# Layer-1 attention: projections over four PSUM banks, spreading products and their copies in the MLP

## The chip, the cores and the metric

The kernel runs on one core of a Trainium2 chip. The metric is the device time of one execution, in microseconds (us). The engines are PE (TensorE), ACT (ScalarE), DVE (VectorE), POOL (GpSimd) and SP (which issues DMAs).

## The reference

Two transformer layers on x of 16 sequences x 512 tokens x 256 features, each stage added to x: linear attention with a memory, a routed MLP, the stage of this document, and a top-1 routed MLP. The stage of this document, for each sequence (`LN` is a layer norm):

```
h  = LN(LN(x)) * ln1_g + ln1_b
q, k, v = heads(h @ WQ + bQ), heads(h @ WK + bK), heads(h @ WV + bV)   # 16 heads of 16
attn = softmax(q k^T / 4, causal, window of 128 keys)
u = h @ Bw;  s_t = A * s_(t-1) + u_t;  ssm = s @ Cw                    # 64 states
g = sigmoid(h @ Wg + bg)
x1 = LN(x) + g * ((attn v) @ WO + bO) + (1 - g) * ssm
out = x + x1 + gelu(LN(x1) @ W1 + b1) @ W2 + b2                        # 1024 hidden
```

## The kernel before, in words

The stage is attn1_phase. Each engine has its own program, written out by hand; the order within an engine is the order of the code, and engines wait for each other by semaphores (`pe.wait_ge(q4_ready, ...)`; `after` is the same, left out where its value isn't positive). A loop `body(it)` runs over 16 sequences. Products in float32 are made of three products of halves, a hi and a lo part each (the helper `three`, lines 72 to 74): wherever PE's result is used as an operand again, ACT copies the hi part out of PSUM and DVE makes the lo part by a subtraction. In what follows that pair is called a split.

PE's body for one sequence has these parts:
- Score steps n = 0 to 31, two heads by 128 queries each. scores(n) writes a mask and q k^T into one of the two banks of s_ps; DVE takes the maximum (maxima), ACT the exponential (exp, two heads, each with a sum), POOL normalises (normalise), PE transposes three steps later (transposes), ACT copies (pT_copy), and PE multiplies by v two steps after that (values). scores(n) waits for exp(n - 2). Steps 0 to 7 have 128 keys, the others 256. After n = 17, 25, 33 and at the end stands a mix: output projection and state product of 128 tokens, 14 products, which ACT copies and POOL gates into x1.
- Spreading. scores needs q and k of a head alone in its rows: spread_qk(j), j = 0 to 7, multiplies q and k by 0/1 matrices, two products for each (hi and lo), into two banks of ab_ps; ACT copies q (q4_copy), DVE copies k (k4_copy). spread_qk 0 and 1 stand ahead of step 0, the others in steps 0 to 5, each ahead of its scores. One bank for each of q and k: spread_qk(j) waits for the copies of j - 1.
- After the scores, for the next sequence: h_transposes, four queries_keys (q and k by halves of 128 features), four values_gates (by 128 tokens, v and gate in one product), and state_input, followed by DVE's scan over the tokens. They use ab_ps[0] and ab_ps[1] in turn, so each waits for the split or eviction of the one before the last.
- h2_transposes after the second layer norm: DVE statistics (stats2_of, norm2), POOL the deviation (inverse_deviation2), DVE normalises (h2n_of).
- The MLP: eight chunks of 128 hidden features. mlp1(m) writes ab_ps[m % 2], ACT applies gelu and copies hi, DVE makes lo, mlp2(m) adds into y_ps, which is the same memory as s_ps. mlp1 runs two chunks ahead. Then DVE adds y to the residual (result_of, four parts).

ACT evaluates the gate's tanh (gates) at the start of a sequence's body, then loads the table for the exponential.

Of the kernel before, what the change touches and what calls it, by code (L numbers as in the profile page):

```python
# [1305 lines left out]
def attn1_phase(nc, x, out, wqk_d, wvg_d, bw_d, cw_d, wo_d, w1_d, w2_d, spread_d, cols_d, rows_d, b1_d, a_d, window_d, half_d, ident_d):  # L1306
# [7 lines left out]
    with ExitStack() as ctx:  # L1314
# [110 lines left out]
        y_ps = s_ps[:].rearrange("p s h k -> p (s h) k")  # L1425

# [187 lines left out]
        def _(act):  # L1614
# [9 lines left out]
            def qk_hi(it, a, m):  # L1624

                act.wait_ge(q_in_psum, (it * 2 + a) * DC + 2 - m)

                after(act, k4_in_psum, it * PAIRS1)
                nc.scalar.activation(qk_hl[a][0][:, m], ab_ps[:, m], ACT.Identity, bias=(bq, bk)[a][:, m:m + 1]).then_inc(qhi_ready, 1)

            def q4_copy(it, j):
                act.wait_ge(q4_in_psum, it * PAIRS1 + j + 1)
                after(act, s_ready, it * NS)
                nc.scalar.copy(q4[:, j], ab_ps[:, 0]).then_inc(q4_ready, 1)
# [69 lines left out]
            projections(0)  # L1704

            def body(it):
                gates(it)

                nc.scalar.activation(table[:], b1[:, 0:1], ACT.Exp)
                q4_copy(it, 0)  # L1710
                q4_copy(it, 1)
                for n in range(NS + LAG_T):
                    if n + 2 < PAIRS1:
                        q4_copy(it, n + 2)
# [20 lines left out]
                for c in range(DC):  # L1735
                    h2_hi(it, c)
                for m in range(MF):
                    gelu(it, m)
                    ff_hi(it, m)

# [3 lines left out]
        def _(dve):  # L1744
# [37 lines left out]
            def qk_lo(it, a, m):  # L1782

                dve.wait_ge(qhi_ready, (it * 2 + a) * DC + 2 - m)
                nc.vector.scalar_tensor_tensor(qk_hl[a][1][:, m], ab_ps[:, m], (bq, bk)[a][:, m:m + 1], qk_hl[a][0][:, m].bitcast(F32), ALU.add, ALU.subtract).then_inc(qlo_ready, 1)

            def values_gates(it, t):
# [5 lines left out]
                nc.vector.tensor_tensor(v[:, t, :, 0:DH1], heads(ab_ps[:, t % 2, 0:D]), heads(rows[:, 0]), ALU.add)  # L1793
                nc.vector.tensor_tensor(gate[:, t], ab_ps[:, t % 2, D:2 * D], rows[:, 1], ALU.add).then_inc(vg_ready, 1)

            def k4_copy(it, j):
                dve.wait_ge(k4_in_psum, it * PAIRS1 + j + 1)
                after(dve, s_ready, it * NS)
                nc.vector.tensor_copy(k4[:, j], ab_ps[:, 1]).then_inc(k4_ready, 1)
# [70 lines left out]
            def projections(it, part):  # L1870
                if part == 0:
                    for a, m in ((0, 0), (1, 1), (1, 0)):
                        qk_lo(it, a, m)
                    values_gates(it, 0)
                    values_gates(it, 1)
                else:
                    values_gates(it, 2)
                    values_gates(it, 3)
                    scan(it)

# [6 lines left out]
            qk_lo(0, 0, 1)  # L1887
            projections(0, 0)
            projections(0, 1)
# [867 lines left out]
```

## Time and profile before

| | us |
|---|---|
| median of 3 runs | 5219.56 (5172.9 to 5221.64) |
| the profiled execution | 5248.13 |
| its span | 5246.3 |
| mean granted TensorE clock | 0.928 |
| PE busy | 4322.6 (82%) |
| DVE, ACT, POOL busy | 2994.6, 2465.0, 2300.0 |

The stage of this change runs from about 2655 to 4880 us of the span. Busy time of different engines overlaps; idle time counts only where it is on the way to the end. A clock of 1.00 is 2.4 GHz, 0.50 is 1.2 GHz.

### The profile page before, as it was taken

What the parts mean: (1) busy time and instruction counts of PE and PEld (TensorE: products, weight loads), DVE (VectorE), ACT (ScalarE), POOL (GpSimd) and SP (SyncE); (2) the same over time, 40 slices, a digit from 0 to 9 for tenths busy, and PEclk for the clock granted to TensorE, in tenths of its full rate; (3) what the DMA queues carried; (4) which work ended last, traced back from release to release, by engine and by line L of the source; (5) the groups of instructions that cost most, each with busy time, mean ns of one, the idle gap of its engine ahead of it and who ended that gap; (6) DMA issues with size and microseconds to landing.
All of it is one profiled execution on the core that took longest, in us unless ns stands there. A gap on an engine that the chain in (4) does not pass through costs nothing. (4 is left out here: it accounts for less than half of the span.)

```text
span 5246.3 us, 152203 instructions
## 1 busy us (share of the span) xinstructions
PE 4322.6 (82%) x61044; PEld 3367.0 (64%) x61140; DVE 2994.6 (57%) x7226; ACT 2465.0 (47%) x5553; POOL 2300.0 (44%) x2391
## 2 busy tenths in 40 slices
PE   3888898888888868888858988888888888888556
PEld 3776776676677757777746666566666656666555
DVE  3777777777767657777654344444444444443444
ACT  3554545554544423323325455555555555555334
POOL 4666666666656400000004444444444444443443
PEclk8999999999999989999979799899999989999579
DMA  2212212222221110000010000000000000000332
GB/s 82 52 44 62 64 47 56 65 49 53 63 56 44 42 51 17 24 24 16 24 60 9 1 8 8 8 8 8 8 8 8 8 8 8 8 8 5 120 96 91
DMA packets 151975, 186.91 MB, mean 36 GB/s; under 512 B 28254, under 2 KB 112353, under 8 KB 149985
## 3 DMA queue, kind: packets, MB, share of 16 engines
q1 hardware_dynamic: 144528, 160.98, 11.4%
q0 software_dynamic: 6864, 17.99, 0.9%
q8 instruction: 388, 6.36, 0.5%
q14 instruction: 195, 1.59, 0.1%
HBM read 68.48 MB, written 44.19 MB: 21 GB/s over the span
## 5 line engine op out<-in xcount | busy, mean ns | idle before, releaser
L1571 POOL TENSOR_TENSOR c_prob<-c_prob,c_inv 128x512 f32<-128x512 f32 (+1 forms) x512 | 484.1, 952 | 825.8 <-DVE c_inv L1824 807.5
L1654 ACT ACTIVATE c_prob<-c_s_ps,c_nmax 128x256 f32<-128x256 f32 (+1 forms) x1024 | 454.2, 453 | 312.0 <-DVE c_nmax L1819 304.9
L1819 DVE TENSOR_REDUCE c_nmax<-c_s_ps 128x2 f32<-128x512 f32 (+1 forms) x512 | 317.4, 620 | 404.8 <-PE c_s_ps L2021 401.6
L848 POOL TENSOR_TENSOR a_swap<-a_swap,a_sin 128x512 f32<-128x512 f32 x128 | 203.0, 1586 | 563.0 <-DMA a_swap<-a_raw 563.0
L2033 PE MATMUL c_t_ps<-c_ident,c_prob 128*128 128x128 f32 x1792 | 321.6, 298 | 14.3 <-POOL c_prob L1571 12.7
L889 ACT COPY a_raw<-a_w_ps 128x512 f32<-128x512 f32 x256 | 150.3, 587 | 350.4 <-PE a_w_ps L74 350.0
L212 POOL TENSOR_TENSOR b_var<-b_mv,b_eps 128x4 f32<-128x4 f32 x16 | 8.5, 533 | 695.4 <-DVE b_mv L304 695.3
L1665 ACT COPY c_pT<-c_t_ps 128x512 f32<-128x512 f32 (+1 forms) x512 | 276.7, 540 | 56.9 <-PE c_ab_ps L2051 55.0
L1170 PE MATMUL a_w_ps<-a_mem,a_sT 64*32 64x65 f32 x14848 | 216.2, 226 | 100.3 <-issue 96.8
L2021 PE MATMUL c_s_ps<-c_k,c_q 64*128 64x256 f32 (+1 forms) x1024 | 257.8, 333 | 22.8 <-issue 20.1
L1170 PEld LDWEIGHTS a_w_ps<-a_mem,a_sT 64*32 64x32 f32 x14848 | 170.2, 106 | 152.1 <-issue 131.1
L1860 DVE TENSOR_TENSOR c_ff_lo<-c_ff,c_ff_hi 128x512 fp32r<-128x512 f32 x128 | 88.6, 692 | 299.9 <-ACT c_ff_hi L1695 299.9
L252 ACT ACTIVATE b_s_sb<-b_gu_ps 128x512 f32<-128x512 f32 x144 | 86.1, 598 | 368.2 <-PE b_gu_ps L74 368.2
L72 PE MATMUL a_w_ps<-a_xT_hi,a_wqk_hi 128*128 128x512 f32 x512 | 237.2, 463 | 20.9 <-DVE a_x_ln L968 12.9
L72 PE MATMUL b_y_ps<-b_wd_hi,b_h_hi 128*128 128x256 f32 x576 | 176.7, 307 | 93.9 <-DVE b_acc L406 47.2
L2033 PEld LDWEIGHTS c_t_ps<-c_ident,c_prob 128*128 128x128 f32 x1792 | 196.9, 146 | 83.1 <-POOL c_prob L1571 16.6
L72 PE MATMUL b_gu_ps<-b_xT_hi,b_wgu_hi 128*128 128x512 f32 x576 | 234.2, 407 | 10.7 <-DVE b_xT_lo L373 10.7
L73 PE MATMUL b_gu_ps<-b_xT_hi,b_wgu_lo 128*128 128x512 f32 x576 | 232.1, 403 | 0.0
L2021 PEld LDWEIGHTS c_s_ps<-c_k,c_q 64*128 64x128 f32 x1024 | 157.9, 193 | 112.4 <-issue 97.1
L74 PE MATMUL b_gu_ps<-b_xT_lo,b_wgu_hi 128*128 128x512 f32 x576 | 229.8, 399 | 0.0
L73 PE MATMUL a_w_ps<-a_xT_hi,a_wqk_lo 128*128 128x512 f32 x512 | 220.0, 430 | 2.8 <-issue 2.8
L74 PE MATMUL a_w_ps<-a_xT_lo,a_wqk_hi 128*128 128x512 f32 x512 | 219.4, 429 | 3.4 <-issue 3.2
(377 smaller groups left out, 13836.9 us busy)
## 6 DMA issues: line engine op xcount, KB each, us to landing
a_swap<-a_raw SPq DMA_DIRECT2D x1024, 64.0 KB, 2.1
d_xb<-sorted_rows SPq DMA_DIRECT2D x71, 130.0 KB
a_x_ln<-x SPq DMA_DIRECT2D x128, 64.0 KB, 2.1
a_acc<-x SPq DMA_DIRECT2D x64, 128.0 KB, 2.8
after_attn<-a_acc SPq DMA_DIRECT2D x64, 128.0 KB, 2.4
b_x_in<-after_attn SPq DMA_DIRECT2D x16, 512.0 KB, 4.4
after_ffn<-b_acc SPq DMA_DIRECT2D x16, 512.0 KB, 3.2
c_x_in<-after_ffn SPq DMA_DIRECT2D x16, 512.0 KB, 4.2
```

What stands on the lines that cost most here:

```text
L72: nc.tensor.matmul(out, w[0], x[0], start=start, stop=False, **options)
L73: nc.tensor.matmul(out, w[1], x[0], start=False, stop=False, **options)
L74: return nc.tensor.matmul(out, w[0], x[1], start=False, stop=stop, **options)
L848: nc.gpsimd.tensor_tensor(q_sw, q_sw, table(sin), ALU.mult)
L889: (rawq_ready, rawk_ready)[a].by(nc.scalar.copy(raw[:, m % 3, a], bank))
L1170: ins = nc.tensor.matmul(into[s * SEG:(s + 1) * SEG, r, j], sT[d, (n // T * T + j) % (2 * PU), a, tok], mem[d, s, j], start=True, stop=True)
L1571: nc.gpsimd.tensor_tensor(p, p, inv[:, n % 4].unsqueeze(2).to_broadcast([P, 2, KB])[:, :, keys_of(i)], ALU.mult).then_inc(norm_ready, 1)
L1654: last = nc.scalar.activation(prob[:, n % 4, h, keys_of(i)], s_ps[:, n % 2, h, keys_of(i)], ACT.Exp, bias=nmax[:, n % 4, h:h + 1], accum_o ...
L1665: nc.scalar.copy(pT[:, n % 2, :, b[0]:2], t_ps[:, n % 2, :, b[0]:2]).then_inc(pT_ready, 1)
L1819: nc.vector.tensor_reduce(nmax[:, n % 4], s_ps[:, n % 2, :, keys_of(i)], AX.X, ALU.max, negate=True).then_inc(max_ready, 1)
L2021: last = nc.tensor.matmul(s_ps[:, n % 2, h, keys_of(i)], q4[r4, slot, i * P:(i + 1) * P], k4[r4, slot, keys_], start=False, stop=(h == 1), ...
L2033: last = nc.tensor.transpose(t_ps[:, n % 2, h, b], prob[:, n % 4, h, b * P:(b + 1) * P], ident[:])
```

## The change

- in_ps: the four query/key products and the four values_gates products use four banks in turn, ab_ps[1], ab_ps[0] and the two banks of s_ps, which the scores have left by then.
- The spreading products use two other banks, o_ps for q and c_ps for k. Those of the next sequence are issued in the MLP: j = 0 ahead of mlp1(0), 1 to 5 after the chunks m = 0 to 4, 6 and 7 after m = 6 and 7. Their copies stand at the same places on ACT and DVE. For the first sequence all eight stand ahead of the loop.
- gates (tanh) of the next sequence stands after chunk 6 of the MLP, the table load for the exponential before the last q4_copy.
- On DVE, splits and evictions of the next sequence are spread between the steps of the second layer norm; on PE, state_input now stands ahead of h2_transposes, and values_gates 2 and 3 behind them.
- scores 0 waits for two of the four results of the sequence before, scores 1 for all.

The diff, with context and the loss of one helper (DVE's projections) left out; "more" is "not last_step(it)":

```diff
@@ -1423,6 +1423,11 @@
 y_ps = s_ps[:].rearrange("p s h k -> p (s h) k")
+s_bank = [s_ps[:, k].rearrange("p h k -> p (h k)") for k in range(2)]
+in_ps = [ab_ps[:, 1], ab_ps[:, 0], s_bank[0], s_bank[1]]
+in_order = ((0, 1), (0, 0), (1, 1), (1, 0))
+q4_ps = o_ps[:]
+k4_ps = c_ps[:].rearrange("p a d -> p (a d)")
...
@@ -1626,12 +1631,12 @@
         after(act, k4_in_psum, it * PAIRS1)
-        nc.scalar.activation(qk_hl[a][0][:, m], ab_ps[:, m], ACT.Identity, bias=(bq, bk)[a][:, m:m + 1]).then_inc(qhi_ready, 1)
+        nc.scalar.activation(qk_hl[a][0][:, m], in_ps[in_order.index((a, m))], ACT.Identity, bias=(bq, bk)[a][:, m:m + 1]).then_inc(qhi_ready, 1)
...
         after(act, s_ready, it * NS)
-        nc.scalar.copy(q4[:, j], ab_ps[:, 0]).then_inc(q4_ready, 1)
+        nc.scalar.copy(q4[:, j], q4_ps).then_inc(q4_ready, 1)
...
@@ -1702,16 +1707,13 @@
     projections(0)
+    for j in range(PAIRS1):
+        q4_copy(0, j)
+    gates(0)
+    nc.scalar.activation(table[:], b1[:, 0:1], ACT.Exp)
     def body(it):
-        gates(it)
-        nc.scalar.activation(table[:], b1[:, 0:1], ACT.Exp)
-        q4_copy(it, 0)
-        q4_copy(it, 1)
         for n in range(NS + LAG_T):
-            if n + 2 < PAIRS1:
-                q4_copy(it, n + 2)
...
@@ -1734,9 +1736,20 @@
             h2_hi(it, c)
+        if not last_step(it):
+            q4_copy(it + 1, 0)
...
             ff_hi(it, m)
+            if not last_step(it):
+                if 1 <= m < MF - 2:
+                    q4_copy(it + 1, m)
+                if m == MF - 2:
+                    gates(it + 1)
+        if not last_step(it):
+            q4_copy(it + 1, PAIRS1 - 2)
+            nc.scalar.activation(table[:], b1[:, 0:1], ACT.Exp)
+            q4_copy(it + 1, PAIRS1 - 1)
...
@@ -1782,7 +1795,7 @@
         dve.wait_ge(qhi_ready, (it * 2 + a) * DC + 2 - m)
-        nc.vector.scalar_tensor_tensor(qk_hl[a][1][:, m], ab_ps[:, m], (bq, bk)[a][:, m:m + 1], qk_hl[a][0][:, m].bitcast(F32), ALU.add, ALU.subtract).then_inc(qlo_ready, 1)
+        nc.vector.scalar_tensor_tensor(qk_hl[a][1][:, m], in_ps[in_order.index((a, m))], (bq, bk)[a][:, m:m + 1], qk_hl[a][0][:, m].bitcast(F32), ALU.add, ALU.subtract).then_inc(qlo_ready, 1)
...
@@ -1790,13 +1803,13 @@
         heads = lambda ap: ap.rearrange("p (h e) -> p h e", e=DH1)
-        nc.vector.tensor_tensor(v[:, t, :, 0:DH1], heads(ab_ps[:, t % 2, 0:D]), heads(rows[:, 0]), ALU.add)
-        nc.vector.tensor_tensor(gate[:, t], ab_ps[:, t % 2, D:2 * D], rows[:, 1], ALU.add).then_inc(vg_ready, 1)
+        nc.vector.tensor_tensor(v[:, t, :, 0:DH1], heads(in_ps[t][:, 0:D]), heads(rows[:, 0]), ALU.add)
+        nc.vector.tensor_tensor(gate[:, t], in_ps[t][:, D:2 * D], rows[:, 1], ALU.add).then_inc(vg_ready, 1)
...
         after(dve, s_ready, it * NS)
-        nc.vector.tensor_copy(k4[:, j], ab_ps[:, 1]).then_inc(k4_ready, 1)
+        nc.vector.tensor_copy(k4[:, j], k4_ps).then_inc(k4_ready, 1)
...
@@ -1884,17 +1886,18 @@
         h_lo(0, c)
-    qk_lo(0, 0, 1)
-    projections(0, 0)
-    projections(0, 1)
+    for part in in_order:
+        qk_lo(0, *part)
+    for t in range(T):
+        values_gates(0, t)
+    scan(0)
+    for j in range(PAIRS1):
+        k4_copy(0, j)
...
         order.step(it)
-        k4_copy(it, 0)
-        k4_copy(it, 1)
+        more = not last_step(it)
         for n in range(NS + 1):
-            if n + 2 < PAIRS1:
-                k4_copy(it, n + 2)
...
@@ -1917,24 +1920,40 @@
         ao_lo(it, T - 1)
-        if not last_step(it):
+        if more:
...
         stats2_of(it, T - 2)
-        if not last_step(it):
-            projections(it + 1, 0)
+        if more:
+            qk_lo(it + 1, 0, 0)
+            qk_lo(it + 1, 1, 1)
...
         norm2(it)
+        if more:
+            qk_lo(it + 1, 1, 0)
+            values_gates(it + 1, 0)
         h2n_of(it)
-        if not last_step(it):
-            projections(it + 1, 1)
+        if more:
+            values_gates(it + 1, 1)
+            scan(it + 1)
...
             affine(it, c, tab[c], h2T, ln2_g, ln2_b, h2T_in_psum, h2T_ready)
+        if more:
+            values_gates(it + 1, 2)
...
             h2_lo(it, c)
+        if more:
+            values_gates(it + 1, 3)
+            k4_copy(it + 1, 0)
...
             ff_lo(it, m)
+            if more and 1 <= m < MF - 2:
+                k4_copy(it + 1, m)
+        if more:
+            k4_copy(it + 1, PAIRS1 - 2)
...
             result_of(it, t)
+        if more:
+            k4_copy(it + 1, PAIRS1 - 1)
...
@@ -1955,7 +1974,7 @@
             pe.wait_ge(hn_ready, it + 1)
-            after(pe, k4_ready, it * PAIRS1)
+            after(pe, ff_ready, (it - 1) * MF)
...
@@ -1965,15 +1984,16 @@
-    def queries_keys(it, a, m):
-        if a:
-            pe.wait_ge(qlo_ready, it * 2 * DC + (2 - m))
-        elif m:
+    def queries_keys(it, n):
+        a, m = in_order[n]
+        if n == 0:
             pe.wait_ge(hlo_ready, (it + 1) * DC)
-        else:
+        elif n == 1:
             after(pe, aolo_ready, it * T)
-        feature_major(wqk, slice(a * D + m * P, a * D + (m + 1) * P), hT_hl, ab_ps[:, m]).then_inc(q_in_psum, 1)
+        elif n == 2:
+            after(pe, exp_ready, it * NS)
+        feature_major(wqk, slice(a * D + m * P, a * D + (m + 1) * P), hT_hl, in_ps[n]).then_inc(q_in_psum, 1)
...
@@ -1981,23 +2001,21 @@
-            pe.wait_ge(vg_ready, (it + 1) * T)
-            after(pe, ff_ready, it * MF)
-        for a, (full, free) in enumerate(((q4_in_psum, q4_ready), (k4_in_psum, k4_ready))):
+            pe.wait_ge(qlo_ready, (it + 1) * 2 * DC)
+        for a, (bank, full, free) in enumerate(((q4_ps, q4_in_psum, q4_ready), (k4_ps, k4_in_psum, k4_ready))):
...
                 pe.wait_ge(free, it * PAIRS1 + j)
+            elif a:
+                pe.wait_ge(state_ready, it + 1)
             for half_ in range(2):
-                last = nc.tensor.matmul(ab_ps[:, a], spread[:, jj, 2 * a + half_], qk_hl[a][half_][:, c], start=(half_ == 0), stop=(half_ == 1))
+                last = nc.tensor.matmul(bank, spread[:, jj, 2 * a + half_], qk_hl[a][half_][:, c], start=(half_ == 0), stop=(half_ == 1))
...
     def values_gates(it, t):
-        if t < 2:
-            pe.wait_ge(qlo_ready, (it * 2 + 1) * DC + 2 - t)
-        else:
-            pe.wait_ge(vg_ready, it * T + t - 1)
+        pe.wait_ge(qlo_ready, it * 2 * DC + t + 1)
...
         for c in range(DC):
-            last = three(nc, ab_ps[:, t % 2], [h[:, c, tok] for h in hT_hl], [w[:, c] for w in wvg], c == 0, c == DC - 1)
+            last = three(nc, in_ps[t], [h[:, c, tok] for h in hT_hl], [w[:, c] for w in wvg], c == 0, c == DC - 1)
...
@@ -2010,7 +2028,9 @@
             pe.wait_ge(k4_ready, it * PAIRS1 + 2 * (n // 2) + 2)
-        if n == 0:
+        if n == 0 and not first_step(it):
+            pe.wait_ge(result_ready, it * T - T // 2)
+        elif n == 1:
...
@@ -2041,10 +2061,12 @@
-            if i == 1:
+            if i == 0:
                 pe.wait_ge(q4_ready, (it + 1) * PAIRS1)
+            elif i == 1:
+                after(pe, ff_ready, it * MF)
             else:
-                after(pe, aolo_ready, it * T + i - 1)
+                pe.wait_ge(aolo_ready, it * T + i - 1)
...
@@ -2058,6 +2080,7 @@
             pe.wait_ge(statelo_ready, it + 1)
+            pe.wait_ge(k4_ready, (it + 1) * PAIRS1)
...
@@ -2077,7 +2100,8 @@
         if m < 2:
-            pe.wait_ge(vg_ready, (it + 2) * T if not last_step(it) else NSEQ * T)
+            if not last_step(it):
+                pe.wait_ge(vg_ready, (it + 1) * T + 2)
...
@@ -2086,8 +2110,10 @@
-            pe.wait_ge(exp_ready, (it + 1) * NS)
+            if last_step(it):
+                pe.wait_ge(exp_ready, NSEQ * NS)
+            else:
+                pe.wait_ge(vg_ready, (it + 2) * T)
...
@@ -2096,18 +2122,17 @@
         h_transposes(0, c)
-    for a, m in ((0, 1), (0, 0), (1, 1), (1, 0)):
-        queries_keys(0, a, m)
+    for n in range(2 * DC):
+        queries_keys(0, n)
...
     state_input(0)
+    for j in range(PAIRS1):
+        spread_qk(0, j)
     def body(it):
-        spread_qk(it, 0)
-        spread_qk(it, 1)
+        more = not last_step(it)
         for n in range(NS + LAG_P):
-            if n + 2 < PAIRS1:
-                spread_qk(it, n + 2)
...
@@ -2118,26 +2143,28 @@
                 h_transposes(it + 1, (n - 27) // 3)
-        if not last_step(it):
-            queries_keys(it + 1, 0, 1)
+        if more:
+            queries_keys(it + 1, 0)
         mix(it, T - 1)
-        if not last_step(it):
-            queries_keys(it + 1, 0, 0)
-            queries_keys(it + 1, 1, 1)
-            queries_keys(it + 1, 1, 0)
+        if more:
+            for n in range(1, 2 * DC):
+                queries_keys(it + 1, n)
...
             values_gates(it + 1, 1)
+            state_input(it + 1)
+        h2_transposes(it)
+        if more:
             values_gates(it + 1, 2)
-        h2_transposes(it)
-        if not last_step(it):
             values_gates(it + 1, 3)
-            state_input(it + 1)
+            spread_qk(it + 1, 0)
...
                 mlp1(it, m + 2)
+            if more and m != MF - 3:
+                spread_qk(it + 1, m + 1 if m < MF - 3 else m)
```

## Rows read from the trace of the kernel before

**Rows 1.** Busy time by window, three stretches of one sequence; columns in its first line.

```profile
core 0: us, PE busy (x) PEld busy (x) DVE busy (x) ACT busy (x) POOL busy (x), PEclk, DMA share, GB/s
...
3637.30:3669.70 32.40, 23.41 (x91) 17.35 (x89) 13.76 (x30) 7.95 (x12) 16.19 (x20) 0.84 0.00 0
3669.70:3690.40 20.70, 19.94 (x132) 18.10 (x133) 4.84 (x7) 9.47 (x15) 0.00 (x0) 1.00 0.00 1
3690.40:3695.80 5.40, 3.51 (x15) 1.91 (x13) 2.71 (x6) 3.72 (x6) 0.00 (x0) 1.00 0.48 138
```

**Rows 2.** Timeline, ACT: start us, length us, operation; the tanh of six of 16 sequences.

```profile
2746.92 1.06 ACT L1639 ACTIVATE c_gate<-c_gate 128x1024 f32<-128x1024 f32 x1 [7.53 <-DVE c_gate L1794]
...
3028.44 1.06 ACT L1639 ACTIVATE c_gate<-c_gate 128x1024 f32<-128x1024 f32 x1 [2.27 <-issue]
...
3288.35 1.06 ACT L1639 ACTIVATE c_gate<-c_gate 128x1024 f32<-128x1024 f32 x1 [2.21 <-issue]
...
3430.83 1.06 ACT L1639 ACTIVATE c_gate<-c_gate 128x1024 f32<-128x1024 f32 x1 [1.95 <-issue]
...
3690.09 1.06 ACT L1639 ACTIVATE c_gate<-c_gate 128x1024 f32<-128x1024 f32 x1 [1.95 <-issue]
...
4740.31 1.05 ACT L1639 ACTIVATE c_gate<-c_gate 128x1024 f32<-128x1024 f32 x1
```

**Rows 3.** Busy time by window, the three long stretches at the low clock.

```profile
2897.00:2950.00 53.00, 51.68 (x228) 30.59 (x229) 17.48 (x47) 26.50 (x84) 26.22 (x32) 0.50 0.00 1
3312.00:3342.00 30.00, 29.15 (x130) 17.78 (x132) 9.91 (x29) 14.12 (x46) 15.47 (x21) 0.51 0.00 0
4234.00:4262.00 28.00, 27.18 (x118) 16.29 (x118) 9.15 (x27) 13.53 (x43) 14.98 (x20) 0.50 0.00 0
```

**Rows 4.** Timeline, PE, from projections to MLP; idle time before and releaser in brackets.

```profile
3637.31 0.50 PE L72 MATMUL c_ab_ps<-c_hT_hi,c_wqk_hi 128*128 128x512 f32 x1
...
3647.27 0.50 PE L72 MATMUL c_ab_ps<-c_wvg_hi,c_hT_hi 128*128 128x512 f32 x1 [1.56 <-DVE c_k_lo L1785]
...
3654.81 1.26 PE L1949 MATMUL c_t_ps<-c_ident,c_y 128*128 128x128 f32 x8 [3.07 <-DVE c_y L1851]
...
3664.44 0.79 PE L72 MATMUL c_ab_ps<-c_h2T_hi,c_w_hi 128*128 128x512 f32 x1 [4.19 <-DVE c_h2T_lo L1856]
```

**Rows 5.** Timeline, POOL and DVE, the work between the last mix and the MLP.

```profile
3644.22 0.74 POOL L1585 TENSOR_TENSOR c_y<-c_t,c_y 128x256 f32<-128x256 f32 x1
...
3651.05 0.42 DVE L1832 BATCH_NORM_STATS2 c_stats<-c_y 128x6 f32<-128x256 f32 x1
...
3653.30 1.38 DVE L1851 TENSOR_SCALAR c_y<-c_y,c_mv,c_lnt 128x256 f32<-128x256 f32 x4 [1.41 <-POOL c_lnt L1549]
...
3662.90 1.41 DVE L1856 TENSOR_TENSOR c_h2T_lo<-c_hT,c_h2T_hi 128x512 fp32r<-128x512 f32 x2
```

**Rows 6.** Timeline, PE, from the end of the MLP into the scores.

```profile
3690.42 0.40 PE L1990 MATMUL c_ab_ps<-c_q_hi,c_spread 128*128 128x512 f32 x1
...
3690.66 0.39 PE L1990 MATMUL c_ab_ps<-c_q_lo,c_spread 128*128 128x512 f32 x1
...
3693.20 0.50 PE L1990 MATMUL c_ab_ps<-c_q_hi,c_spread 128*128 128x512 f32 x1 [1.68 <-ACT c_q L1634]
...
3695.76 0.28 PE L2017 MATMUL c_s_ps<-c_maskb,c_identb 128*128 128x256 bf16 x1
...
3706.27 0.28 PE L2017 MATMUL c_s_ps<-c_maskb,c_identb 128*128 128x256 bf16 x1
...
3710.48 0.44 PE L2033 MATMUL c_t_ps<-c_ident,c_prob 128*128 128x128 f32 x2 [0.81 <-POOL c_prob L1571]
```

**Rows 7.** Timeline, DVE and ACT, the results and the first score step.

```profile
3690.62 1.42 DVE L1866 TENSOR_TENSOR c_res<-c_s_ps,c_res 128x256 f32<-128x256 f32 x4 [1.76 <-PE c_s_ps L74]
...
3696.56 0.41 DVE L1819 TENSOR_REDUCE c_nmax<-c_s_ps 128x2 f32<-128x256 f32 x1
...
3697.09 0.37 ACT L1654 ACTIVATE c_prob<-c_s_ps,c_nmax 128x128 f32<-128x128 f32 x1 [1.12 <-DVE c_nmax L1819]
```

More of the change, by code:

```diff
@@ L1868, in _ @@
             tab = [t_ps[:, c].rearrange("p h b q -> p (h b q)") for c in range(DC)]
[L1870 to L1875, printed above, removed]
-                else:
-                    values_gates(it, 2)
-                    values_gates(it, 3)
-                    scan(it)
             norm(0)
@@ L1982, in spread_qk @@
                 if j == 0:
-                    pe.wait_ge(vg_ready, (it + 1) * T)
-                    after(pe, ff_ready, it * MF)
-                for a, (full, free) in enumerate(((q4_in_psum, q4_ready), (k4_in_psum, k4_ready))):
+                    pe.wait_ge(qlo_ready, (it + 1) * 2 * DC)
+                for a, (bank, full, free) in enumerate(((q4_ps, q4_in_psum, q4_ready), (k4_ps, k4_in_psum, k4_ready))):
                     if j:
                         pe.wait_ge(free, it * PAIRS1 + j)
+                    elif a:
+                        pe.wait_ge(state_ready, it + 1)
                     for half_ in range(2):
-                        last = nc.tensor.matmul(ab_ps[:, a], spread[:, jj, 2 * a + half_], qk_hl[a][half_][:, c], start=(half_ == 0), stop=(half_ == 1))
+                        last = nc.tensor.matmul(bank, spread[:, jj, 2 * a + half_], qk_hl[a][half_][:, c], start=(half_ == 0), stop=(half_ == 1))
                     last.then_inc(full, 1)
             def values_gates(it, t):
-                if t < 2:
-                    pe.wait_ge(qlo_ready, (it * 2 + 1) * DC + 2 - t)
-                else:
-                    pe.wait_ge(vg_ready, it * T + t - 1)
+                pe.wait_ge(qlo_ready, it * 2 * DC + t + 1)
                 tok = slice(t * P, (t + 1) * P)
                 for c in range(DC):
-                    last = three(nc, ab_ps[:, t % 2], [h[:, c, tok] for h in hT_hl], [w[:, c] for w in wvg], c == 0, c == DC - 1)
+                    last = three(nc, in_ps[t], [h[:, c, tok] for h in hT_hl], [w[:, c] for w in wvg], c == 0, c == DC - 1)
                 last.then_inc(vg_in_psum, 1)
```

## The prediction

> **What bounds the kernel now.** The page says that PE is busy 82% of the span; its chain of waits covers the last phase alone and says nothing here. So I went to the layer-1 attention by windows, which show what each part of a sequence leaves idle [rows 1]. A sequence has four parts: 32 score steps (n = 0 to 31), projections with the second layer norm, the MLP, and a start in which spreading products and their copies alternate. The MLP is PE's own: 19.94 us busy of 20.70. The part ahead of it is not: 23.41 of 32.40, at a clock of 0.84. The start is not: 3.51 of 5.40 [rows 1].
>
> The timeline names the waits. PE idles 1.56 us for the split of the last key projection, because values_gates reuses its bank, then 3.07 us for the normalised x1 and 4.19 us for the split of h2 [rows 4]. The 3.07 us are a matter of queue order: the last x1 is written at 3644.22 + 0.74 = 3644.96, but DVE takes its statistics only at 3651.05, behind splits and two evictions of the next sequence [rows 5]. At the start PE waits 1.68 us for a copy [rows 6], behind ACT's tanh and table load.
>
> The clock is the second bound. One sequence, tanh to tanh, takes (3690.09 - 3430.83) / 2 = 129.6 us; the mean of fifteen is (4740.31 - 2746.92) / 15 = 132.9 [rows 2]. The difference is three stretches of 28 to 53 us at a clock of 0.50, the lower of the two levels (1.2 GHz, against 2.4), with PE 97% busy in them [rows 3]. The short one at 3312 makes its sequence 3430.83 - 3288.35 = 142.5 us, so costs 12.9; the long one at 2897 makes two sequences 281.5 us, so costs 22.3 [rows 2, 3].
>
> **The change, part by part, at full clock.** One sequence, times from the one that starts its projections at 3637.31 [rows 4].
>
> 1. Projections and norm. Four banks take away the bank waits: four query/key products, the last mix, two value/gate products and the state input run on without a gap, to about 3649.3. On DVE the statistics of the last x1 now stand behind two splits, so run at about 3645.4, not 3651.05. Aggregates and POOL's deviation take as long as before (3651.05 to 3653.30, so 2.25 us): 3647.7. The fourth split and one eviction stand ahead of the normalising, which starts at 3647.9, takes 1.38 and ends at 3649.3 [rows 5]. Transposes start at 3649.4, not 3654.81: 5.4 us earlier. Behind them DVE has one eviction and the scan (2.0), two affines (1.5), an eviction (0.75), two splits (1.41), about 5.6 us in all, against 3664.44 - 3654.81 = 9.6 now. PE covers this with the last two value/gate products and spreading product 0. The MLP starts at 3655.0 instead of 3664.44: **9.4 us gained**, sized by the durations in the rows, bounds 7 and 10.
> 2. First hidden products. Now 12 of them take from 3664.44 to 3669.7, since the clock fell in the idle time. At 0.24 us each [rows 6] they take 2.9, and then PE waits about 0.8 for gelu and split, which the low clock hid: **1.6 gained**.
> 3. MLP. Six of the seven pairs of spreading products that move here fall inside its 20.7 us. A pair is four products of 0.24, so 0.93 to 0.96. All are exposed because PE has no gap here but 0.76 (the 20.70 - 19.94) [rows 1, 6]: 6 x 0.93 - 0.76 = **4.8 lost**. ACT gets one 0.59 us copy and DVE one 0.69 us copy for each of PE's 3.7 us, against 1.3 and 0.7 us of own work: both fit. If the tanh in the midst of the gelus made ACT load its table again, 1.28 us twice a sequence would cost up to 15 x 2.6 = 38 us; today's tanh follows the gelus with idle time and no load ahead of it [rows 2], so I take nothing, and keep 38 for the range.
> 4. Start. From MLP end to the mask of score step 6: 3706.27 - 3690.42 = 15.85 us now [rows 6]. After: spreading pair 7 takes 0.95; scores 0 start then, but DVE first adds four results (to 1.62) and copies k4 (to 2.2), so the first maximum is ready at 2.6 and exp 0 at 3.5 (0.41 and four ACT pieces of some 0.8) [rows 7]. Scores n waits for exp n - 2, which ACT does at about one per us: steps 2, 3, 4, 5, 6 at 3.6, 4.4, 5.7, 6.6, 7.9. **7.9 gained**. The first table load and tanh, 2.5 us, now hide under mlp2.
>
> Sum: 9.4 + 1.6 - 4.8 + 7.9 = 14.1 us a sequence: 129.6 becomes 115.5. The prologue pays: eight pairs one after another with a copy between them and then tanh and table load, about 3 us net. SP's loads start earlier; POOL's residuals too, and nobody waits for them. Fifteen transitions: 15 x 14.1 - 3 = 209 us, if the clock stays as it is.
>
> **What the thinner start does to the clock.** What PE did before each long low stretch: nothing unusual. It had come from score steps 8 and 9, where it waits once, for 0.81 us [rows 6], and this place is the same in all sequences; three of them fell and the others held. Score steps hold the clock only just: they use half or a quarter of the array, masks and scores of the first eight are 128 and 256 wide. Once low, the clock came back only at a mix, whose 14 products are dense: twice at the first (n = 17), once at the second. Today's start has idle time as well (1.68 us, [rows 6]) and held, but it carries 12 dense spreading products in 5.4 us [rows 1]. The changed start carries none after its first microsecond: by step 4 of the working, PE has some 3.2 us of work, all of it narrow, between 1.0 and 6.6. That is much thinner than the place that already fell three times. I take it that the clock falls in nine of ten starts and stays low until a mix.
>
> A rule speaks to this on each side. The Trainium skill, TensorE: Matmul & The Clock Gate, "A second HAM failure mode: psum-queue depth-cycling", describes PE idling briefly and often between groups until the clock oscillates; by that rule the result is the 5270 below. The same page, "HAM oscillation — how this bites in real kernels", lays the fall to one long idle gap; by that rule the start holds and the result is 5010. The trace has three falls behind a gap of only 0.81 us, so it sides with the first.
>
> Price of a fall: the stretch starts near step 4 or 5, not 10. Five more steps of 1.3 to 2.0 us become 2.0 to 2.5 at half clock, 3.3 us in all, on top of 12.9 (first mix) or 22.3 (second) [rows 2]: 16.2 or 25.6, at two to one 19.3. Bounds for one start: 0 and 25.6; nothing of it can be a gain. A sequence is 115.5 + 0.9 x 19.3 = 132.9, exactly today's mean. The first start of the phase falls too, 16, and the prologue's 3 stay: +19. From the profiled execution's 5248.1 us this is 5267. That execution is 28.6 us above the median of 5219.56 (runs 5172.9 to 5221.6), which two long stretches more would explain; the changed kernel falls nearly always and has no such luck to lose, so I forecast its median at **5270**, not 29 less.
>
> **Rivals.**
> - *Gain eaten by the clock* (forecast), 0.70. Own range: all falls end at the first mix, 15 x 3.1 less, 5225; all at the second, 5365. For it: the three stretches and their ends [rows 3]. Against it: today's start holds.
> - *The clock holds in the start*, 0.18, the other side: 5219.6 - 209 = 5010. It decides between scores 1 and step 6 of each sequence: if PE's narrow work there is enough, nothing of the 14.1 is given back. Break-even is 14.1 us a sequence, so about three falls in four starts.
> - *It falls and comes back early*, 0.12: at a cost of some 7 us a start (half of the gain), 5219.6 - 15 x 7 = 5115 to 5165.
> - *The change does not do what it says*: the MLP's start bound by DVE's serial work, 9.4 becoming 5.4. Adds 60 us to any of these; in the bounds.
>
> **How the numbers follow.** A measurement of this kernel tells about 1% (52 us) from no change. The forecast case has half its chance above 5272 (0.36) and half within 1% (0.34). The other two are faster, 0.30, with little of the early return inside 1%: faster 0.29, same 0.34, slower 0.37. The range leaves out the holding clock and the far ends: 5060 to 5365. The forecast's own range is 5225 to 5365.
>
> **What would show it.** By windows, the MLP with the next spreading products at about 25.5 us and PE nearly full; first hidden product 17 to 18 us after the first projection; scores 0 within 1.5 us of the last mlp2; a clock of 0.50 from about step 4 to step 17 or 25 in most sequences, with steps of 2.0 to 3.4 us. Sequences of 115 us with a clock near 1.00 would prove me wrong and the rival right; a DVE wait ahead of the MLP as long as now would show step 1 wrong.

## The result, and the profile after

| | before | after |
|---|---|---|
| median (lowest to highest) of four runs each on one chip, us | 5197.77 (5172.9 to 5221.64) | 5356.62 (5321.03 to 5376.43) |
| profiled execution, us | 5248.13 | 5321.03 |
| mean granted clock | 0.928 | 0.870 |
| layer-1 attention, first projection to the next phase's first product on PE, us | 2149.6 | 2253.2 |

The changed kernel is slower: ratio 1.0299, 95% interval 1.0211 to 1.0386. Ratios leave out executions more than 1.5% above the fastest of the same kernel, which here are two of the ten of e2. The forecast was 5270 with 5060 to 5365 around it; the sign was right and the time 87 us short. As a change that is more: 50 us above the 5219.56 known then was forecast, and 159 us above 5197.77 was measured. Page of the kernel after, its first lines and the clock's line of section 2:

```profile
span 5319.2 us, 152604 instructions
...
PE 4573.6 (86%) x61140; PEld 3492.3 (66%) x61140; DVE 2992.0 (56%) x7226; ACT 2484.6 (47%) x5553; POOL 2319.6 (44%) x2391
...
PEclk8999999999999899999967787888788868887569
```

PE's share went up from 82% to 86% in a kernel that got slower: a clue that its work is being stretched, not added. The clock's digits say where: 6 to 8 over the layer-1 attention, the second half of the line but for its last three digits. Those (569) belong to the next phase and are nearly the same before (579).

First the full-clock work of one sequence, as the timeline shows it. PE from the first projection to the first product of mlp2:

```profile
3649.76 0.50 PE L72 MATMUL c_ab_ps<-c_hT_hi,c_wqk_hi 128*128 128x512 f32 x1
...
3667.03 0.50 PE L72 MATMUL c_ab_ps<-c_h2T_hi,c_w_hi 128*128 128x512 f32 x1 [0.50 <-DVE c_h2T_lo L1869]
...
3671.07 0.38 PE L72 MATMUL c_s_ps<-c_w_hi,c_ff_hi 128*128 128x256 f32 x1 [0.99 <-DVE c_ff_lo L1873]
```

And DVE, the statistics of the last x1 and the normalising:

```profile
3657.76 0.42 DVE L1845 BATCH_NORM_STATS2 c_stats<-c_y 128x6 f32<-128x256 f32 x1
...
3660.00 1.38 DVE L1864 TENSOR_SCALAR c_y<-c_y,c_mv,c_lnt 128x256 f32<-128x256 f32 x4
```

The wait of 4.19 us ahead of the first hidden product [rows 4] is 0.50 now, and that product comes 17.3 us after the first projection instead of 27.1. The statistics stand 8.0 us behind the first projection, where the working had 8.1.

By windows: the rest of the MLP with its spreading products, and the low stretches behind this sequence's start and behind the next:

```profile
core 0: us, PE busy (x) PEld busy (x) DVE busy (x) ACT busy (x) POOL busy (x), PEclk, DMA share, GB/s
...
3671.10:3696.50 25.40, 25.40 (x157) 22.51 (x158) 9.00 (x13) 13.38 (x21) 0.93 (x1) 1.00 0.00 0
3701.10:3776.20 75.10, 73.88 (x311) 42.77 (x312) 24.19 (x69) 37.69 (x131) 35.24 (x45) 0.50 0.02 7
3847.90:3892.30 44.40, 43.73 (x178) 24.55 (x178) 14.53 (x46) 23.68 (x89) 23.38 (x32) 0.50 0.02 7
```

The MLP is as dense as it can be. From 3701.10 on the clock is 0.50 for 75 us, in the next sequence for 44. In the layer-1 stage there are 15 such stretches of 44 to 99 us, one behind each start from the second on, where the kernel before had three [rows 3]. Eleven last 44 to 49 us and end at the first mix, two 72 to 75 us and end at the second. The two of 98 to 99 us end ahead of the third mix, among transposes and products with v: four transposes take 1.12 us and, 1.9 us later, 0.66, and the mix comes only then:

```profile
3238.62 1.12 PE L2053 MATMUL c_t_ps<-c_ident,c_prob 128*128 128x128 f32 x4
...
3240.53 0.66 PE L2053 MATMUL c_t_ps<-c_ident,c_prob 128*128 128x128 f32 x4
...
3241.69 0.39 PE L2086 MATMUL c_c_ps<-c_cw_hi,c_state_hl 128*128 128x256 f32 x1
```

PE in the start that falls:

```profile
3698.36 0.27 PE L2037 MATMUL c_s_ps<-c_maskb,c_identb 128*128 128x256 bf16 x1
...
3702.32 0.40 PE L2037 MATMUL c_s_ps<-c_maskb,c_identb 128*128 128x256 bf16 x1 [3.33 <-ACT c_prob L1659]
```

The same 256-column mask takes 0.27 us at 3698.36 and 0.40 at 3702.32: the fall lies in the 3.33 us wait for the first exponentials. So it is in 13 starts, with waits of 3.32 to 3.61 us. The second start and the last wait only 1.02 us there and fall two steps later. DVE shows why that wait is longer than its work:

```profile
3696.69 1.42 DVE L1879 TENSOR_TENSOR c_res<-c_s_ps,c_res 128x256 f32<-128x256 f32 x4 [0.82 <-PE c_s_ps L74]
3698.02 0.68 DVE L1812 CAST c_k<-c_c_ps 128x512 fp32r<-128x512 f32 x1
3700.93 0.76 DVE L1832 TENSOR_REDUCE c_nmax<-c_s_ps 128x2 f32<-128x256 f32 x2 [2.22 <-issue]
```

Ahead of the first maximum, DVE stands 2.22 us for nothing that the profile shows ("issue"). This is where the loop over sequences turns; the second start and the last, which stand behind no turn, are without it. Last, the tanh on ACT, which marks the sequences:

```profile
2727.80 1.06 ACT L1644 ACTIVATE c_gate<-c_gate 128x1024 f32<-128x1024 f32 x1
...
2854.06 1.05 ACT L1644 ACTIVATE c_gate<-c_gate 128x1024 f32<-128x1024 f32 x1
...
3691.31 1.05 ACT L1644 ACTIVATE c_gate<-c_gate 128x1024 f32<-128x1024 f32 x1
...
3837.39 1.05 ACT L1644 ACTIVATE c_gate<-c_gate 128x1024 f32<-128x1024 f32 x1
...
4800.64 1.05 ACT L1644 ACTIVATE c_gate<-c_gate 128x1024 f32<-128x1024 f32 x1
```

From the second tanh on, the mean sequence is (4800.64 - 2854.06) / 14 = 139.0 us, where 132.9 was forecast. The value of 132.9 for the kernel before [rows 2] is the mean of all fifteen, which is (4800.64 - 2727.80) / 15 = 138.2 here. The one at 3691.31, with the 75 us stretch, is 146.1.

### The profile page after: what moved, and what is told of

It reads as the page before. It is cut to its first block and busy times, and to the rows that moved or that the text cites. A ratio compares the mean times of both kernels' runs of the same rounds, so it can differ in the third digit from the quotient of the medians.

```text
span 5319.2 us, 152604 instructions
## 1 busy us (share of the span) xinstructions
PE 4573.6 (86%) x61140; PEld 3492.3 (66%) x61140; DVE 2992.0 (56%) x7226; ACT 2484.6 (47%) x5553; POOL 2319.6 (44%) x2391
## 5 line engine op out<-in xcount | busy, mean ns | idle before, releaser
L2053 PE MATMUL c_t_ps<-c_ident,c_prob 128*128 128x128 f32 x1792 | 412.3, 361 | 1.3
L2041 PE MATMUL c_s_ps<-c_k,c_q 64*128 64x256 f32 (+1 forms) x1024 | 332.0, 415 | 0.0
L2041 PEld LDWEIGHTS c_s_ps<-c_k,c_q 64*128 64x128 f32 x1024 | 212.2, 257 | 162.6 <-issue 157.9
L2053 PEld LDWEIGHTS c_t_ps<-c_ident,c_prob 128*128 128x128 f32 x1792 | 245.8, 177 | 88.6 <-issue 54.3
L2037 PE MATMUL c_s_ps<-c_maskb,c_identb 128*128 128x512 bf16 (+1 forms) x512 | 242.6, 474 | 58.9 <-ACT c_prob L1659 56.6
```

The costliest lines, as they stand in the source:

```text
L2037: nc.tensor.matmul(s_ps[:, n % 2, :, keys_of(i)], identb[:], maskb[:, :, keys_of(i)], start=True, stop=False, skip_group_check=True)
L2041: last = nc.tensor.matmul(s_ps[:, n % 2, h, keys_of(i)], q4[r4, slot, i * P:(i + 1) * P], k4[r4, slot, keys_], start=False, stop=(h == 1), ...
L2053: last = nc.tensor.transpose(t_ps[:, n % 2, h, b], prob[:, n % 4, h, b * P:(b + 1) * P], ident[:])
```

## The experiments

Each ratio is to the kernel before, run beside that experiment; its median there lay between 5195 and 5227 us. Between experiments, ratios and the lengths of sequences say more than differences of some 30 us between times.

Two theories stood at first. A: the clock falls in the start because PE has too little work there; work added there brings the 14 us a sequence back. B: the moved work itself costs what was seen (the MLP, a queue). Under A two readings: busy time counts, or the width of the products does. "Fill" is a dense product (128 x 128 weights, 512 columns) into a free bank that nobody reads; it adds work and leaves the output as it is. In all experiments but e5 it is

```
def fill(it, count):
    for k in range(count):
        nc.tensor.matmul(ab_ps[:, 1], spread[:, 0, 0],
                         qk_hl[0][0][:, 0], start=True, stop=True)
```

**e1_fill.** The kernel after, with 19 fills in the start of each sequence.

```diff
+                    if n in {1: 8, 2: 3, 3: 3, 4: 2, 5: 2, 6: 1}:
+                        fill(it, {1: 8, 2: 3, 3: 3, 4: 2, 5: 2, 6: 1}[n])
```

> The changed kernel, with 19 products of 512 columns added to each sequence's start that nobody reads (into the free bank ab_ps[1]): 8 after scores 1, then 3, 3, 2, 2 and 1 after scores 2 to 6. The output stays. Theory A (the thin start loses the clock): no long stretch at 0.50 starts in the start any more; a sequence, tanh to tanh, goes from 139.0 us to about 118 (115.5 worked out for full clock, and 2.2 for DVE's gap ahead of the first maximum), so 15 x 21 = 315 us less than 5356.6: about 5040. Theory B (the loss is a wait or a queue in the new order, the clock is a by-product): the 19 products, 4.5 us a sequence, only come on top where PE wasn't idle: 5360 to 5430, with or without the low clock.

Measured: 5054.36 us (5049.45 to 5060.64), ratio to before 0.971 (0.9634 to 0.9786), clock 0.947. More work, and 302 us less than the kernel after. B is out: the moved work is still there and cost nothing of the kind. Sequences take 118 to 123 us and have no long low stretch. By windows, the start of one:

```profile
3706.80:3709.00 2.20, 2.11 (x10) 1.60 (x11) 0.76 (x2) 0.48 (x3) 0.00 (x0) 0.98 0.78 217
3709.00:3712.90 3.90, 3.90 (x13) 2.44 (x11) 0.66 (x3) 1.29 (x7) 0.84 (x2) 0.57 0.22 74
3712.90:3716.00 3.10, 3.10 (x17) 2.15 (x16) 0.99 (x4) 1.98 (x12) 1.25 (x3) 1.00 0.03 5
```

The clock does fall here for about 3 us, as in about half of the starts behind a turn, after a wait at the loop's turn, and it is back while the fills run:

```profile
3706.89 0.28 PE L2037 MATMUL c_s_ps<-c_maskb,c_identb 128*128 128x256 bf16 x1 [2.68 <-issue]
```

**e5_narrow.** As e1, each fill replaced by four narrow bf16 products (32 weight columns, 128 columns): similar busy time, a small part of the array.

```diff
-                for k in range(count):
-                    nc.tensor.matmul(ab_ps[:, 1], spread[:, 0, 0], ...)
+                for k in range(4 * count):
+                    nc.tensor.matmul(ab_ps[0:ROWS, 1, 0:P], identb[:, 0:ROWS],
+                                     maskb[:, 0, 0:P], start=True, stop=True)
```

> As e1_fill, at the same six places, but each dense product is replaced by four narrow ones (32 weight columns, 128 moving columns, bfloat16), which keep PE busy for about as long (4 x 0.06 us) with little work. Theory A1 (idle time is what loses the clock; being busy is enough): as e1_fill, about 5050, no long low stretch. Theory A2 (what counts is how much of the array works, not how long PE is busy): the clock falls in nearly every start as without any fill, 5356 or, with the added time, up to 5420.

Measured, one run: 5076.57 us, clock 0.939. Two starts fell for long (78.5 and 47.8 us), the others took 118.2 to 122.9 us. Being busy with narrow products was enough in 13 of 15 starts; the two falls leave room for a part of width, which one run can't size.

**e4_burst.** The kernel after with 18 fills behind score step 8, none in the start.

```diff
+                    if n in {8: 18}:
+                        fill(it, {8: 18}[n])
```

> The changed kernel, with 18 unread dense products after scores 8. The start stays thin. Theory A: the clock falls in the start as before, but comes back in or right behind the dense products, at steps 8 to 9 rather than at the first mix (17) or later: low stretches of 15 to 25 us, not 44 to 99. The products cost 7.7 us at the low clock (18 x 0.43) and give back about 0.41 us for each us at full clock: 5260 to 5330. Theory B (only the mix, or time, brings the clock back): stretches as long as now and 16 x 7.7 us more, 5440 to 5480.

Measured, one run: 5150.92 us, 109 us below the range expected; why it gives back so much more isn't shown. Each start falls as before, and the low stretch ends inside the burst, here after 17.1 us, by windows and on PE's timeline:

```profile
3383.90:3401.00 17.10, 16.26 (x56) 9.67 (x57) 5.43 (x18) 8.94 (x41) 7.73 (x12) 0.50 0.16 46
```
```profile
3397.74 5.95 PE L2125 MATMUL c_ab_ps<-c_q_hi,c_spread 128*128 128x512 f32 x18
```

So dense work ends a fall too, and the mixes in the kernel after do what this burst does, later, in 13 of its 15 stretches. Holding the clock (e1) is worth 97 us more than bringing it back.

**e11_gap_only.** The kernel after with 8 fills behind scores 1 alone, which cut the longest wait.

```diff
+                    if n in {1: 8}:
+                        fill(it, {1: 8}[n])
```

> The changed kernel with 8 unread dense products after scores 1 only, so that the 3.3 us idle gap is filled and the thin steps 2 to 6 are as in the change. If the gap alone loses the clock: no long low stretch from the start, about 5050 as e1_fill. If the thin steps alone are enough: the clock falls one place later, at steps 3 to 6, in most sequences, 5250 or more. A fall in some sequences would say that both are near the edge.

Measured, one run: 5310.13 us, clock 0.877. PE's timeline through the new place of the fall, and the window behind it:

```profile
3134.51 2.14 PE L2125 MATMUL c_ab_ps<-c_q_hi,c_spread 128*128 128x512 f32 x8
3137.98 0.28 PE L2037 MATMUL c_s_ps<-c_maskb,c_identb 128*128 128x256 bf16 x1 [1.33 <-ACT c_prob L1659]
...
3140.15 0.28 PE L2037 MATMUL c_s_ps<-c_maskb,c_identb 128*128 128x256 bf16 x1 [0.46 <-ACT c_prob L1659]
3140.36 0.59 PE L2041 MATMUL c_s_ps<-c_k,c_q 64*128 64x128 f32 x2
```
```profile
3140.50:3181.40 40.90, 39.96 (x167) 22.89 (x170) 13.26 (x40) 21.08 (x75) 22.04 (x30) 0.50 0.00 0
```

In this start the clock survives the first wait, 1.33 us now, and falls two steps later. The 13 starts behind a turn all fall so, with a first wait of 1.25 to 1.60 us. The three that stand behind no turn wait 0.58 us at most and hold through step 5: the first has no low stretch, the second falls only at steps 8 and 9, the last at step 6. In e1 the clock fell after 2.68 us too, but came back in 3 us. So the first wait is not all that counts; what follows it decides how long the clock stays low, and in this kernel the turn still helps to bring it down.

**e8_unroll.** The kernel after with two sequences in one turn of the loop (seven turns for fourteen sequences).

```diff
-            with eng.Fori(1, NSEQ - 1) as it:
-                body(it)
+            with eng.Fori(0, NSEQ // 2 - 1) as turn:
+                body(turn * 2 + 1)
+                body(turn * 2 + 2)
```

> The changed kernel with two sequences in each turn of the loop. In it DVE waits 2.22 us with no releaser ahead of its first maximum. If the turn is the cause, this goes in every second sequence: 7 x 2.2 = 15 us less, some 5340, and since the start is then less thin by 2.2 us the clock may fall a little later; low stretches stay in nearly every sequence. If the gap were why the clock falls, half of the low stretches would go: 5356 - 7 x 20 = about 5215.

Measured: 5281.43 us (5269.35 to 5317.94), ratio 1.0108 (1.0041 to 1.0176): 75 us under the kernel after, where seven turns less at the 2.22 us of DVE's row are 16. All 15 falls stay, but 12 of them last about 44 us and end at the first mix, three end at the second, and none lasts longer. Nine starts stand behind no turn; in these no wait is longer than 1.02 us, and they fall all the same:

```profile
3561.01 0.28 PE L2038 MATMUL c_s_ps<-c_maskb,c_identb 128*128 128x256 bf16 x1 [1.02 <-ACT c_prob L1660]
...
3563.18 0.40 PE L2038 MATMUL c_s_ps<-c_maskb,c_identb 128*128 128x256 bf16 x1 [0.21 <-ACT c_prob L1660]
```

The turn is thus not why the clock falls in the thin start. The tanh rows give its price, and that of a fall:

```profile
2865.31 1.06 ACT L1645 ACTIVATE c_gate<-c_gate 128x1024 f32<-128x1024 f32 x1
...
3008.79 1.06 ACT L1645 ACTIVATE c_gate<-c_gate 128x1024 f32<-128x1024 f32 x1
...
3552.32 1.06 ACT L1645 ACTIVATE c_gate<-c_gate 128x1024 f32<-128x1024 f32 x1
...
3684.55 1.06 ACT L1645 ACTIVATE c_gate<-c_gate 128x1024 f32<-128x1024 f32 x1
...
3818.82 1.06 ACT L1645 ACTIVATE c_gate<-c_gate 128x1024 f32<-128x1024 f32 x1
```

With a fall to the first mix, a sequence takes 132.2 us inside a turn and 134.3 across one; in the mean of six of each kind the turn makes 1.8 us; with a fall to the second mix, inside a turn, 143.5.

**e7_fill_unroll.** e1 and e8 together.

> e1_fill with two sequences in each turn of the loop (7 turns, not 14); nothing else. In e1_fill PE idles 2.68 us ahead of scores 0 with no releaser, at the place where the loop turns. If the turn is the cause: the gap stands only ahead of every second sequence, 7 x 2.5 = 17 us less, 5054 to about 5037. If it is a wait of the new order (results, copies): a gap in every sequence and 5054.

Measured: 5029.8 us (5018.1 to 5043.38), ratio 0.9611 (0.9557 to 0.9665). Between two sequences of one turn the start is that of the working, PE first, then DVE:

```profile
3694.73 0.40 PE L2012 MATMUL c_o_ps<-c_q_hi,c_spread 128*128 128x512 f32 x1
...
3699.14 0.28 PE L2038 MATMUL c_s_ps<-c_maskb,c_identb 128*128 128x256 bf16 x1
```
```profile
3696.27 0.68 DVE L1813 CAST c_k<-c_c_ps 128x512 fp32r<-128x512 f32 x1
3696.86 0.92 DVE L1833 TENSOR_REDUCE c_nmax<-c_s_ps 128x2 f32<-128x256 f32 x2
```

The maximum follows the copy without the 2.22 us, and step 2 stands 4.4 us behind the last mlp2, fills included, instead of 5.8.

**e9_lean, e10_lean7.** Fewer fills (12), and two (e9, as in e8) or seven (e10) sequences in a turn.

```diff
+                    if n in {1: 4, 2: 2, 3: 2, 4: 1, 5: 1, 8: 1, 9: 1}:
+                        fill(it, {1: 4, 2: 2, 3: 2, 4: 1, 5: 1, 8: 1, 9: 1}[n])
```

> e7_fill_unroll with fewer unread dense products, since there PE reached scores 2 at 4.4 us behind the last mlp2 though exp 0 was ready for it at 3.6: 4 after scores 1, 2, 2, 1, 1 after scores 2 to 5, and one each after scores 8 and 9. If the clock still holds, a sequence inside a turn goes from 118.2 to about 116.5 us: 5030 - 15 x 1.7 = about 5005. If 19 were needed, some starts lose the clock again, for 16 to 25 us each: 5030 to 5250.

> e9_lean with seven sequences in each of two turns of the loop. In e7_fill_unroll a sequence behind a turn took 120.8 to 123.3 us, one inside 118.2: five turns fewer, 5 x 3.9 = 19 us less than e9_lean, so about 4985 if that holds 5005. If a longer program is fetched more slowly, nothing gained or some us lost.

Measured: e9 5124.1 us (5114.84 to 5135.34), ratio 0.9844 (0.9779 to 0.9908); e10 **4999.3** us (4978.68 to 5002.43), ratio 0.9591 (0.9528 to 0.9655), the lowest time here, though its interval overlaps those of e7 and e6. In e9 the starts inside a turn hold the clock, the six behind a turn lose it, all to the first mix. The tanh rows of e9, one sequence of each kind, and its low stretch:

```profile
3344.45 1.06 ACT L1645 ACTIVATE c_gate<-c_gate 128x1024 f32<-128x1024 f32 x1
...
3483.86 1.06 ACT L1645 ACTIVATE c_gate<-c_gate 128x1024 f32<-128x1024 f32 x1
...
3600.50 1.06 ACT L1645 ACTIVATE c_gate<-c_gate 128x1024 f32<-128x1024 f32 x1
```
```profile
3353.90:3405.10 51.20, 49.79 (x192) 29.23 (x195) 15.26 (x47) 24.39 (x89) 23.39 (x32) 0.50 0.04 12
```

139.4 us with the fall, 116.6 without. In e10, with only one start behind a turn:

```profile
3561.98 1.05 ACT L1645 ACTIVATE c_gate<-c_gate 128x1024 f32<-128x1024 f32 x1
...
3678.67 1.05 ACT L1645 ACTIVATE c_gate<-c_gate 128x1024 f32<-128x1024 f32 x1
...
3798.82 1.05 ACT L1645 ACTIVATE c_gate<-c_gate 128x1024 f32<-128x1024 f32 x1
```

116.7 us inside the turn, 120.2 across it: this one turn costs 3.5 us, some of it through the clock, which dips there for about 3 us. In e10 that start came back at once; the same fills lost the clock in e9. Why the one and not the other stays open.

**e2_banks.** The reordering and the four banks alone; spreading products, their copies and the tanh stay in the start as in the kernel before.

```diff
-        q4_ps = o_ps[:]
-        k4_ps = c_ps[:].rearrange("p a d -> p (a d)")
+        q4_ps = ab_ps[:, 0]
+        k4_ps = ab_ps[:, 1]
```

> One part of the change alone: four banks for the projections, with the new order of splits, evictions, state input and transposes. The spreading products, their copies, the tanh and the table load stay where they were before, in ab_ps. Theory A: the start keeps its dense products and so its clock (a few long low stretches, as before); steps 1 and 2 of the prediction give 9.4 + 1.6 = 11 us a sequence: 5197.8 - 165 = 5033. Theory B (this reordering is what costs: DVE's queue ahead of the MLP): 5200 or more, first hidden product as late as before.

Measured: 5190.09 us (5124.68 to 5276.27, ten runs), ratio 0.9939 (0.9893 to 0.9985): a miss. Undisturbed sequences are as short as expected, 118.8 to 119.8 us, against 129.6 before [rows 2]. But in the profiled execution, its slowest at 5276.27, the clock fell in 11 of 16 sequences, each time at score steps 8 and 9, as the three falls of before [rows 6]. No start lost it: with the spreading products in place the start holds. Why step 9 loses the clock so much more often than in the kernel before, behind the same 0.81 us, stays open. By windows and on PE's timeline:

```profile
3000.90:3086.20 85.30, 85.30 (x376) 50.53 (x377) 27.32 (x69) 40.66 (x127) 40.52 (x49) 0.50 0.00 0
```
```profile
3000.54 0.44 PE L2037 MATMUL c_t_ps<-c_ident,c_prob 128*128 128x128 f32 x2 [0.81 <-POOL c_prob L1576]
```

**e6_banks_fill.** e2 with three fills behind each of scores 8 and 9.

```diff
+                    if n in (8, 9):
+                        fill(it, 3)
```

> e2_banks (four banks alone) with three unread dense products after scores 8 and three after scores 9. In e2_banks 11 of 16 sequences lost the clock behind score steps 8 and 9, and those that did not took 118.8 to 119.8 us. Theory A: this place is the cause; with the fill all sequences take about 120 (119 and six products of 0.24 us, partly in idle time), so 5190 less 15 x (135.9 - 120) = about 4960 to 5030, and runs within 20 us of each other. Theory B (the reordering loses the clock elsewhere or for another reason): as e2_banks, 5190, or 20 more.

Measured: 5035.3 us (5033.54 to 5037.85), ratio 0.9624 (0.9574 to 0.9673), a little above what was expected. All sequences are alike; the tanh of two that lie four apart:

```profile
3332.28 1.06 ACT L1644 ACTIVATE c_gate<-c_gate 128x1024 f32<-128x1024 f32 x1 [2.15 <-issue]
...
3810.52 1.06 ACT L1644 ACTIVATE c_gate<-c_gate 128x1024 f32<-128x1024 f32 x1 [1.94 <-issue]
```

(3810.52 - 3332.28) / 4 = 119.6 us. Six dense products a sequence are worth 155 us to e2 (3.2% by the ratios), and the runs spread over 4 us instead of 151.

**e3_before_fill.** The kernel before with two fills behind each of scores 8 and 9.

```diff
+                    if n in {8: 2, 9: 2}:
+                        fill(it, {8: 2, 9: 2}[n])
```

> The kernel before, with two such unread products after scores 8 and two after scores 9, where PE waits 0.25 and 0.81 us and behind which the clock fell in three of 16 sequences. Theory A: no long low stretch any more; 129.7 us for every sequence, the three stretches' 48 us gone from the profiled execution's 5248 (5200 or less) and the spread of the runs within some 10 us: median 5165 to 5185. Theory B (the falls have nothing to do with what PE does there): as many long stretches as before and up to 16 x 4 x 0.24 = 15 us more: 5200 to 5215.

Measured: 5187.73 us (5174.04 to 5208.93, ten runs), ratio 0.9961 (0.9922 to 1.0001). No long low stretch is left in its trace, the mean of the fifteen sequences is 130.4 us against 132.9, and the runs spread over 35 us instead of 71. As a gain it can't be told from none.

## Why the prediction was right or wrong

- **Steps 1 and 2 (projections, norm, first hidden products): right.** First hidden product 17.3 us after the first projection (17 to 18 said), and 0.99 us of wait ahead of mlp2 (0.8 said).
- **Step 3 (MLP): right.** 25.40 us, all PE, against 25.5. The table rival did not happen: the tanh in the midst of the gelus has no load beside it.
- **Step 4 (start): right but for one term that was left out.** Step 2 was to come 3.6 us after the last mlp2 and came at 5.8 (3702.32 - 3696.49). What is missing is the turn of the loop: before, ACT showed it as 1.95 to 2.27 us of "issue" ahead of the tanh [rows 2], while PE went on with spreading products. I read those rows as idle time that helps the tanh, and did not ask what covers it once the products are gone. It costs 1.8 us between sequences that fall either way (e8) and 3.5 in the one turn of e10.
- **The sum at full clock: right.** 115.5 us forecast; 116.6 in e9 and e10, which still carry 12 fills.
- **The clock: right in kind, short in number.** It falls in all 15 starts behind the first, not in nine of ten, and, as forecast, in the first (granted clock 0.56 between 2728.2 and 2760 us). The price of one fall was right: to the first mix 132.2 - 116.6 = 15.6 us (16.2 forecast), to the second 143.5 - 116.6 = 26.9 (25.6), where the 116.6 still has its 12 fills in it. That there is a longer one, past the second mix, was not foreseen.
- **The total.** Of the fourteen sequences from the second tanh on, ten fall to the first mix (15.6 us each), two to the second (26.9) and two for longer: these take 156.2 us (from 3131.69 to 3287.85, and from 4240.98 to 4397.15), 22.0 above the 134.2 of a first-mix fall, so 37.6. The mean fall is 20.4 us; 116.6 + 20.4 + 1.7 for the turn (1.8 in 13 of 14) make 138.7, measured 139.0. Against the 132.9 forecast, falls are 3.0 short (20.4 against 0.9 x 19.3 = 17.4), the turn 1.7 and the full clock 1.1. Over the stage that is 45 + 23 + 16 = 84 us. The forecast put 19 us on the stage; measured are 2253.2 - 2149.6 = 103.6, so 85 more. The term that was mis-sized most is thus the falls: their number (15 x 0.1 x 19.3 = 29 us) and, with 16, the two that outlast the second mix. The missing turn, 23, comes next. The prices are from one trace each, and what lets two stretches last so long is not shown.
- **The range.** That it held 5356.62 is in part luck: its upper end, 5365, stood for falls that all last to the second mix, and 11 of 15 ended at the first.
- **One reading was wrong.** The long stretch of before was priced by two sequences, 281.5 us, less twice 129.6: 22.3. The tanh between them stands at 2872.30:

```profile
2872.30 1.05 ACT L1639 ACTIVATE c_gate<-c_gate 128x1024 f32<-128x1024 f32 x1
```

The first of the two took 125.4 us and the one with the stretch 156.1, so it cost 26.5. With that the forecast for a fall to the second mix would have been 29.8 where 26.9 was measured; that the 25.6 comes out closer is chance.
- **One reason was wrong where it was used to choose a number.** I took the profiled execution of before to lie 28.6 us above the median because of long stretches. The first projection of layer 1 stands at 2731.06 us there and at 2701.46 in the kernel after, with unchanged code ahead of it; in the 13 profiled executions it lies between 2698 and 2731. That part alone can explain the 28.6.
- **The rivals.** The clock held in none of the starts behind the first; 5010 was what e1 (5054) and e10 (4999) gave once PE was kept busy, so that rival's price was right and its condition was not met. The early return (5115 to 5165) is what e4 brought about: 5150.9.

Of the two sections of the Trainium skill weighed ahead (TensorE: Matmul & The Clock Gate), "A second HAM failure mode: psum-queue depth-cycling" fits better: nine starts of e8 fall where PE idles briefly, 1.02 us at the longest. The other, on one long idle gap, would have had these starts hold the clock, and they did not; in the kernel after, the 3.3 us waits of 13 starts would have suited it too.

What of the change is worth having: the four banks and the order on DVE, 129.6 to 119.6 us a sequence (e6, its six fills included). Moving the spreading products gains nothing by itself, since PE does them at one place or the other: with the clock held and one sequence in a turn, e6 (not moved) has 119.6 us a sequence and e1 (moved) 118 to 123, at ratios of 0.9624 and 0.971. With the turn gone as well and fewer fills, the moved products reach 116.6 us a sequence (e10); e6 with seven sequences in a turn was not run, so how much of these 3 us is due to the move stays open.

## What to carry to other kernels

Products that look hidden in a start that waits for other engines may be what holds TensorE's clock there, and what covers the turn of a loop; ask both before moving them. When a change shortens such a stage, count what work is left on PE between the first wait and the next dense stretch, price a fall by stretches already in the trace, and try a few unread dense products at the thin place as a test: if adding work makes the kernel faster, the clock was the bound. A run-to-run spread as e2's, 3% on one core, was here the sign of a thin place that falls in some sequences and not in others: six fills brought it to 4 us.

## What the runs showed of the hardware

- The clock stays at 0.50 for 44 to 99 us while PE is 97 to 100% busy at that level with narrow scores, transposes and masks. It came back at dense products in most stretches (the burst in e4, a mix in 13 of 15 in the kernel after and in all 15 of e8), but in two of the kernel after 1.5 us ahead of a mix, with none.
- In thin steps the clock falls behind waits of 1.02 us at most (nine starts of e8), and behind one of 0.81 us at step 9 (11 of 16 sequences of e2).
- One turn of the loop shows as 1.95 to 2.97 us of "issue": on ACT in the kernel before, on DVE in the kernel after, on PE in e1. In the length of a sequence it is 1.8 us (e8) to 3.5 us (e10).
- Taking half of the turns out (e8) left the number of low stretches as it was and took away the longest: 12 ended at the first mix and three at the second, where the kernel after had 11, two, and two beyond. Which detail of timing decides where one ends stays open.
